# Moving ten groups of score tiles one place later in the projection stage of a Perceiver layer

## The chip, the cores and the metric

One Trainium2 chip, one of its NeuronCores. The metric is the time of one execution on the device in microseconds (us), the median of several runs. The engines are TensorE (PE; its weight loads are listed as PEld), VectorE (DVE), ScalarE (ACT), GpSimd (POOL) and SyncE (SP), which here only issues DMAs.

## The reference, cut to what matters

The input x is 512 x 512, the context ctx_768 is 8192 x 384. The layer is a cross attention, a local self attention and a feed-forward network with weights rounded to a 4-bit grid, each added to x. The change lies in the first part of the cross attention and in what the kernel does beside it:

```python
def _L0_xattn_ref(x, y, Wq, bq, Wk, bk, Wv, bv, W1, b1, W2, b2):   # y = ctx_768: 8192 rows
    q = (x @ Wq + bq)...                                           # 16 heads of 32 columns
    k = (y @ Wk + bk)...
    v = (y @ Wv + bv)...
    scores = jnp.einsum('bnhd,bmhd->bhnm', q, k) * scale
    attn = jax.nn.softmax(scores, axis=-1)                         # needs a bound of each row's maximum
    ...
def fp4_quant_dequant(x):                                          # for the weights of the last part
    scale = jnp.maximum(jnp.max(jnp.abs(xb), axis=-1, keepdims=True) / 6.0, 1e-12)   # blocks of 16
    q = _GRID[jnp.searchsorted(_MID, jnp.abs(xb / scale))] * jnp.sign(xb / scale) * scale
```

## The kernel before

The kernel is one program with explicit semaphores: each engine has its own list of instructions in a fixed order, and waits (`wait`, `wait_ge`) for counts that other engines raise. The first stage, "project" (lines 285 to 825), computes keys and values for 8192 context rows in 16 blocks (b = 0 to 15) of 512 rows; `two_blocks(i)` handles b = 2i (u = 0, an even block) and b = 2i + 1 (u = 1, an odd block). All operands are split into a high and a low float16 half, so that each product is three matmuls.

For one block TensorE issues, in this order: `keys` (L736): four tiles g = 0 to 3 of nine matmuls (L752); `next_y` (L777): twelve transposes (L710) of the next block's rows into the three PSUM banks of `yT_ps`; `values` (L759): four tiles t = 0 to 3 of nine matmuls (L769 to L771).

Between these stand groups of four "score tiles" (`maxima` of TensorE, L720, matmuls at L732): scores of 128 queries each against 512 keys of an earlier block, of which only the row maxima are wanted. The first three go to the three banks of `yT_ps`, the fourth to `pre_ps`; VectorE's own `maxima` (L646, reductions at L651) reads them out. A table `part_at` says at which place a group stands: KEYS_2 (behind the third key tile), VALUES_1, VALUES_2, VALUES_3 (behind the second, third and fourth tile of values). Twelve blocks, 2 to 4 and on, have a group at VALUES_1; blocks 3, 8 and 10 have a second one, at VALUES_3; block 15 has its two at KEYS_2 and VALUES_2. All groups share the same four banks. So before a group TensorE waits for three things: the stored keys (`k_out`, or `k_in`), `ylo_ready` (VectorE has taken the low half of the next block out of `yT_ps`, `y_low`, L611), and `pre_read`: VectorE has read all tiles of all earlier groups (`done_before`). `next_y` waits for `pre_read` too, for the three tiles in `yT_ps` (L779).

VectorE's list for one block is: four times the low half of a key tile (`key_low`, L607), with three steps of the weight rounding between them and, where the block before had a group at VALUES_3, two of that group's maxima behind each of the first two; `y_low`; two rounding steps (`quantize(2)`, L683); `maxima` of VALUES_1 (L684); two more rounding steps in an even block, three in an odd one (L687). The fifteen rounding steps of two blocks are listed in STEPS (L654): for each of three weight units w: `scales` (L616 to L622), `halves` of the unit before (L642, L643), `rounder` (L627, L629), `add` (L632), `subtract` (L636), and at last `halves` of unit 2. In an even block these are scales 0, rounder 0, add 0 between the keys, subtract 0 and scales 1 before the maxima, halves 0 and rounder 1 behind them; in an odd block add 1, subtract 1, scales 2 between the keys, halves 1 and rounder 2 before the maxima, add 2, subtract 2, halves 2 behind them.

GpSimd does two operations for each unit: `qn` (L497), started by the end of scales and awaited by rounder, and `w_whole` (L503), started by subtract and awaited by halves and by the next unit's scales (L619). ScalarE takes the high halves out of PSUM: `keys_out` (L539, L541), `y_high` (L548), `values_out` (L555). SyncE's queue stores keys, values and rounded weights and loads the next rows; a store of a weight unit waits for `halved` (L430).

Behind the stage stands the attention stage ("attend", from line 850), which begins when the maxima of the first head are complete.

Of the kernel before, what the change touches and what calls it, by code (L numbers as in the profile page):

```python
# [43 lines left out]
NB = M // BLK  # L44
# [87 lines left out]
def perceiver(nc, a, out):  # L132

    with ExitStack() as whole:
# [113 lines left out]
        def layer_norm_vector(dve, chain, var_ready, sd_ready, k, xn, xn_ready, first=0, tiles=range(TT)):  # L248


            for t in range(first, TT):
                chain(nc.vector.bn_stats(stats[:, t, :], x[:, t, :]))
            chain.wait()
            for t in range(TT):
                chain(nc.vector.bn_aggr(mv[:, t, :], stats[:, t, :]))
            chain.wait()
            nc.vector.tensor_scalar(ve[:], mv[:, :, 1], EPS, None, ALU.add).then_inc(var_ready, 1)
            dve.wait_ge(sd_ready, k)
            dve.wait_ge(var_ready, k)
            chain.link(nc.vector.reciprocal(r0[:], sd[:]))  # L260
            chain.link(nc.vector.tensor_tensor(r1[:], r0[:], r0[:], ALU.mult))
            chain.link(nc.vector.tensor_tensor(r2[:], r1[:], ve[:], ALU.mult))
            chain.link(nc.vector.tensor_scalar(r1[:], r2[:], -0.5, 1.5, ALU.mult, ALU.add))
            chain.link(nc.vector.tensor_tensor(r2[:], r0[:], r1[:], ALU.mult))
            for t in tiles:
                nc.vector.tensor_scalar(xn[:, t, :], x[:, t, :], mv[:, t, 0:1], r2[:, t:t + 1],  # L266
                                        ALU.subtract, ALU.mult).then_inc(xn_ready, 1)
# [17 lines left out]
        with ExitStack() as st:  # L285
# [71 lines left out]
            KEYS_2, VALUES_1, VALUES_2, VALUES_3 = range(4)  # L357
            part_at = {(2, VALUES_1): (0, 0), (3, VALUES_1): (0, 1), (3, VALUES_3): (0, 2), (8, VALUES_3): (1, 0),
                       (10, VALUES_3): (1, 1)}
            for b in range(4, NB - 1):  # L360
                part_at[b, VALUES_1] = (0, b - 1)
            part_at[NB - 1, KEYS_2] = (0, NB - 2)
            part_at[NB - 1, VALUES_2] = (0, NB - 1)
            done_before = {at: TT * n for n, at in enumerate(sorted(part_at))}
# [3 lines left out]
            def pre_bank(j):  # L368

                return yT_ps[:, j] if j < TT - 1 else pre_ps[:]  # L370
# [218 lines left out]
            def _(dve):  # L589
# [13 lines left out]
                def key_low(i, u, g):  # L603
                    n = (2 * i + u) * G + g
                    wait(dve, kf_ready, n + 1)
                    wait(dve, khi_ready, n + 1)
                    nc.vector.tensor_tensor(k_lo[:, u, g], kf[:, g % 2], k_hi[:, u, g], ALU.subtract).then_inc(klo_ready, 1)  # L607

                def y_low(i, u):
                    wait(dve, yhi_ready, 2 * i + u + 2)  # L610
                    nc.vector.tensor_tensor(yT_lo[:, 1 - u], yT_ps[:], yT_hi[:, 1 - u], ALU.subtract).then_inc(ylo_ready, 1)  # L611
# [34 lines left out]
                def maxima(b, place, tiles=range(TT)):  # L646
                    if (b, place) in part_at:
                        h, part = part_at[b, place]
                        for j in tiles:
                            dve.wait_ge(pre_ready, done_before[b, place] + j + 1)  # L650
                            nc.vector.tensor_reduce(part_max[:, h, j, part:part + 1], pre_bank(j), AX.X,  # L651
                                                    ALU.max).then_inc(pre_read, 1)
# [6 lines left out]
                def two_blocks(i, last):  # L659
                    steps = iter(STEPS)  # L660

                    def quantize(count):
                        for _ in range(count):
                            part, w = next(steps)
                            part(i, w)

                    def keys(u):
                        b = 2 * i + u
                        for g in range(G):
                            key_low(i, u, g)  # L670
                            if g < 3:
                                quantize(1)
                            maxima(b - 1, VALUES_3, range(2 * g, min(2 * g + 2, TT)))
                        maxima(b, KEYS_2)

                    for u in range(2):
                        if not (last and u == 1):
                            keys(u)
                            if i == 0 and u == 0:
                                dve.wait_ge(x_in, 16)  # L680
                                layer_norm_vector(dve, chain, var_ready, sd_ready, 1, xn_q, xn_ready)
                            y_low(i, u)
                            quantize(2)  # L683
                            maxima(2 * i + u, VALUES_1)  # L684
                            if last:
                                keys(1)
                            quantize(2 + u)  # L687
                            if last:
                                quantize(5)
                                maxima(2 * i + 1, VALUES_2)  # L690
                    assert next(steps, None) is None

                two_blocks(0, False)
                for g in range(G):
                    dve.wait_ge(qf_ready, g + 1)
                    dve.wait_ge(qhi_ready, g + 1)
                    nc.vector.tensor_tensor(q_lo[:, g], qf[:, g], q_hi[:, g], ALU.subtract).then_inc(qlo_ready, 1)
                for i in range(1, NB // 2):
                    two_blocks(i, i == NB // 2 - 1)
# [1606 lines left out]
```

## Time and profile before

| | us |
|---|---|
| median of 3 runs | 1385.35 |
| lowest of them | 1385.23 |
| profiled execution, span from first to last instruction | 1383.2 |
| TensorE busy in the span | 1332.2 |
| VectorE busy | 1120.9 |
| ScalarE busy | 806.1 |
| GpSimd busy | 778.7 |

The profiled execution is given by its span; the median lies 2.15 us above it, which is what lies around the span. An engine's matmuls overlap, so their printed durations (0.38 us) are longer than the distance from one start to the next. In a timeline the bracket at a row's end is the time for which the engine was idle before it and what released it; "issue" is a wait for which the profile shows no releaser.

### The profile page before, as it was taken

To read this page: it belongs to the slowest core of one execution; us is meant where nothing else is said; L and a number is where in the kernel's file an instruction comes from. 1 tells how busy PE (TensorE), PEld (TensorE's weight loads), DVE (VectorE), ACT (ScalarE), POOL (GpSimd) and SP (SyncE) were. 2 spreads that over 40 slices of the span, in tenths; PEclk is the share of its full clock that TensorE was granted. 3 is DMA by queue.
4 is the path that set the end of the run, shared out by engine and by line. 5 is a ranking of instruction groups with operands and counts; after the bars stand their busy time and mean duration, and the time that the engine had idled before them with its cause. 6 is when DMAs were issued, how large, how long until landed. Compare 5 with 4: busy or idle time off the path is not lost. (4 is left out here: it accounts for less than half of the span.)

```text
span 1383.2 us, 39979 instructions
## 1 busy us (share of the span) xinstructions
PE 1332.2 (96%) x17098; PEld 702.8 (51%) x17098; DVE 1120.9 (81%) x1786; ACT 806.1 (58%) x1459; POOL 778.7 (56%) x320
## 2 busy tenths in 40 slices
PE   7999999998999999999999999999999999999898
PEld 4444444443555555555555555545555445566454
DVE  5778888887888888888888888888887746578895
ACT  4454444443777777776777776776777841354332
POOL 0322222122899988988998898899889100201121
PEclk9999999999999999999999999999999999999999
DMA  8568777786352122122212112211210030491000
GB/s 265 177 169 231 207 211 211 210 238 177 91 183 69 39 69 67 30 65 67 69 39 68 56 38 69 67 50 57 59 66 31 5 145 1 92 214 41 0 9 23
DMA packets 127799, 137.54 MB, mean 99 GB/s; under 512 B 44995, under 2 KB 108995, under 8 KB 125699
## 3 DMA queue, kind: packets, MB, share of 16 engines
q1 hardware_dynamic: 127622, 134.98, 34.6%
q8 instruction: 135, 2.21, 0.7%
q14 instruction: 42, 0.34, 0.1%
HBM read 75.70 MB, written 44.17 MB: 87 GB/s over the span
## 5 line engine op out<-in xcount | busy, mean ns | idle before, releaser
L1297 DVE TENSOR_REDUCE early<-attend_banks 128x1 f32<-128x512 f32 x952 | 612.4, 685 | 80.8 <-PE attend_banks L1042 75.6
L1261 ACT ACTIVATE attend_prob<-attend_banks 128x512 f32<-128x512 f32 x1024 | 536.0, 599 | 200.8 <-PE attend_banks L1079 198.6
L1439 POOL TENSOR_TENSOR early<-early,attend_prob 128x1024 f32<-128x1024 f32 x210 | 614.5, 2926 | 37.7 <-ACT attend_prob L1261 9.6
L1079 PE MATMUL attend_banks<-early,k_first 97*32 97x512 f16 x2560 | 258.9, 382 | 3.1 <-ACT attend_prob L1261 3.1
L1042 PE MATMUL attend_banks<-k_first,early 96*32 96x512 f16 x2272 | 235.1, 382 | 1.1 <-PEq L285 1.1
L1079 PE MATMUL attend_banks<-early,attend_k_rest 97*32 97x512 f16 x1536 | 154.1, 381 | 2.8 <-ACT attend_prob L1261 2.8
L1042 PE MATMUL attend_banks<-attend_k_rest,early 96*32 96x512 f16 x1536 | 155.8, 380 | 0.0
L1103 PE MATMUL attend_banks<-attend_prob,ones 128*32 128x128 f32 x3048 | 134.3, 272 | 3.6 <-DVE attend_recip L1309 3.6
L1092 PE MATMUL attend_banks<-attend_prob,wkv_area 128*32 128x512 f32 x1024 | 134.1, 592 | 0.0
L1092 PE MATMUL attend_banks<-attend_prob,attend_vh_odd 128*32 128x512 f32 x1024 | 133.6, 592 | 0.0
L503 POOL TENSOR_TENSOR project_w_whole<-project_grid,project_qscale 128x704 f32<-128x704 f32 x24 | 33.3, 1386 | 173.0 <-DVE project_grid L636 173.0
L1103 PEld LDWEIGHTS attend_banks<-attend_prob,ones 128*32 128x32 f32 x3048 | 95.6, 110 | 54.5 <-DVE attend_recip L1309 11.1
L1079 PEld LDWEIGHTS attend_banks<-early,k_first 97*32 97x32 f16 x2560 | 77.3, 97 | 85.6 <-ACT attend_prob L1261 46.6
L1042 PEld LDWEIGHTS attend_banks<-k_first,early 96*32 96x32 f16 x2272 | 71.3, 97 | 58.4 <-issue 34.9
L555 ACT ACTIVATE project_v<-project_v_ps 128x512 f32<-128x512 f32 x64 | 38.1, 597 | 92.1 <-PE project_v_ps L771 92.1
L497 POOL TENSOR_TENSOR project_qn<-early,project_qinv 128x704 f32<-128x704 f32 x24 | 37.9, 1580 | 87.6 <-issue 50.2
L539 ACT ACTIVATE early<-project_k_ps,project_bk 128x512 f32<-128x512 f32 x64 | 44.0, 688 | 63.6 <-PE project_k_ps L752 61.6
L769 PE MATMUL project_v_ps<-project_w_hi,project_yT_hi 128*128 128x512 f16 x192 | 73.9, 385 | 5.7 <-ACT project_v L555 5.7
L1079 PEld LDWEIGHTS attend_banks<-early,attend_k_rest 97*32 97x32 f16 x1536 | 47.0, 96 | 57.8 <-ACT attend_prob L1261 38.1
L752 PE MATMUL project_k_ps<-project_yT_hi,project_w_hi 128*128 128x512 f16 x192 | 72.5, 379 | 2.3 <-ACT project_q_hi L574 1.4
L770 PE MATMUL project_v_ps<-project_w_lo,project_yT_hi 128*128 128x512 f16 x192 | 73.9, 385 | 0.0
L771 PE MATMUL project_v_ps<-project_w_hi,project_yT_lo 128*128 128x512 f16 x192 | 73.7, 384 | 0.0
(220 smaller groups left out, 1823.6 us busy)
## 6 DMA issues: line engine op xcount, KB each, us to landing
v_scratch<-project_v SPq DMA_DIRECT2D x16, 1024.0 KB, 8.9
early<-in_ctx_dram SPq DMA_DIRECT2D x16, 768.0 KB, 6.2
k_first<-k_scratch SPq DMA_DIRECT2D x36, 256.0 KB, 3.5
k_scratch<-project_k_hi SPq DMA_DIRECT2D x64, 128.0 KB, 2.9
k_scratch<-project_k_lo SPq DMA_DIRECT2D x64, 128.0 KB, 3.1
attend_vh_odd<-v_scratch SPq DMA_DIRECT2D x8, 1024.0 KB, 5.0
wkv_area<-v_scratch SPq DMA_DIRECT2D x7, 1024.0 KB, 4.8
attend_k_rest<-k_scratch SPq DMA_DIRECT2D x24, 256.0 KB, 3.5
```

Source lines behind the costliest of these rows:

```text
L539: nc.scalar.activation(kf[:, g % 2], k_ps[:, g % 2], ACT.Identity, bias=bk[:, g:g + 1], scale=1.0 / WSCALE).then_inc(kf_ready, 1)
L752: last = nc.tensor.matmul(k_ps[:, g % 2], (w_lo if p == 2 else w_hi)[:, 0, k, cols], (yT_lo if p == 1 else yT_hi)[:, u, k], start=(k, p) = ...
L769: nc.tensor.matmul(v_ps[:, t % 2], yT_hi[:, u, k, cols], w_hi[:, 1, k], start=k == 0, stop=False)
L770: nc.tensor.matmul(v_ps[:, t % 2], yT_hi[:, u, k, cols], w_lo[:, 1, k], start=False, stop=False)
L771: last = nc.tensor.matmul(v_ps[:, t % 2], yT_lo[:, u, k, cols], w_hi[:, 1, k], start=False, stop=k == CK - 1)
L1042: last = nc.tensor.matmul(pre_ps[c * HD:(c + 1) * HD, bank, :], q_stack[0:KROWS, h, queries], keys_at(s, part * BLK, (part + 1) * BLK)[0:K ...
L1079: last = nc.tensor.matmul(s_ps[c * HD:(c + 1) * HD, s_bank[n], :], key_rows[:, c * HD:(c + 1) * HD], q_stack[0:KROWS + 1, h, :], start=Tru ...
L1092: last = nc.tensor.matmul(pv_ps[t * HD:(t + 1) * HD, :], vh[s][:, BT * q + t, :], prob[:, q % PSLOTS, t, :], start=q == 0, stop=q == QUADS ...
L1103: last = nc.tensor.matmul(den_ps[t * HD:(t + 1) * HD, 0:P], ones[:], prob[:, q % PSLOTS, n, t * P:(t + 1) * P], start=q == 0 and n == summ ...
L1261: nc.scalar.activation(prob[:, q % PSLOTS, t, :], s_ps[:, s_bank[BT * q + t]], ACT.Exp, scale=SCALE).then_inc(p_ready, 1)
L1297: nc.vector.tensor_reduce(part_max[:, s, j, part:part + 1], pre_ps[:, bank], AX.X, ALU.max).then_inc(pre_read, 1)
L1439: nc.gpsimd.tensor_tensor(sums, sums, prob[:, q % PSLOTS, 0:n], ALU.add).then_inc(pool_summed, 1)
```

## The change

The groups at VALUES_1 in blocks 4 to 13 go to VALUES_2, so that TensorE issues them behind the third tile of values instead of the second. On VectorE their maxima go behind the block's last rounding steps, at the end of its list. The group of block 14 stays at VALUES_1, as do those of blocks 2 and 3, and the groups at VALUES_3 in blocks 3, 8 and 10 stay where they are.

```diff
             part_at = {(2, VALUES_1): (0, 0), (3, VALUES_1): (0, 1), (3, VALUES_3): (0, 2), (8, VALUES_3): (1, 0),
                        (10, VALUES_3): (1, 1)}
-            for b in range(4, NB - 1):
-                part_at[b, VALUES_1] = (0, b - 1)
+            for b in range(4, NB - 2):
+                part_at[b, VALUES_2] = (0, b - 1)
+            part_at[NB - 2, VALUES_1] = (0, NB - 3)
             part_at[NB - 1, KEYS_2] = (0, NB - 2)
             part_at[NB - 1, VALUES_2] = (0, NB - 1)
...
                             quantize(2 + u)
+                            if not last:
+                                maxima(2 * i + u, VALUES_2)
                             if last:
                                 quantize(5)
                                 maxima(2 * i + 1, VALUES_2)
```

## Rows read from the trace of the kernel before

**Rows 1.** Windows: the projection stage and the rest. Columns: us, busy of each engine.
```profile
core 0: us, PE busy (x) PEld busy (x) DVE busy (x) ACT busy (x) POOL busy (x), PEclk, DMA share, GB/s
0.00:343.00 343.00, 316.00 (x1514) 155.51 (x1514) 270.30 (x418) 157.10 (x228) 76.38 (x54) 0.99 0.73 209
343.00:1383.20 1040.20, 1016.17 (x15584) 547.29 (x15584) 850.65 (x1368) 648.96 (x1231) 702.34 (x266) 1.00 0.23 63
```

**Rows 2.** Timeline of TensorE, blocks 5 to 9. Columns: start us, us, operation, idle before.
```profile
137.28 1.47 PE L710 MATMUL project_yT_ps<-ident,early 128*128 128x128 f32 x12
...
155.09 1.47 PE L710 MATMUL project_yT_ps<-ident,early 128*128 128x128 f32 x12
...
161.32 0.81 PE L732 MATMUL project_yT_ps<-k_first,early 96*128 96x512 f16 x3 [0.87 <-issue]
...
191.65 1.47 PE L710 MATMUL project_yT_ps<-ident,early 128*128 128x128 f32 x12
...
203.55 0.81 PE L732 MATMUL project_yT_ps<-k_first,early 96*128 96x512 f16 x3 [0.76 <-DVE early L651]
```

**Rows 3.** Timeline of VectorE, blocks 6 and 8.
```profile
159.47 1.75 DVE L611 TENSOR_TENSOR project_yT_lo<-project_yT_ps,project_yT_hi 128x1536 f16<-128x1536 f32 x1
...
200.92 1.88 DVE L651 TENSOR_REDUCE early<-project_yT_ps 128x1 f32<-128x512 f32 x3
202.72 0.68 DVE L651 TENSOR_REDUCE early<-project_pre_ps 128x1 f32<-128x512 f32 x1
203.31 0.52 DVE L642 TENSOR_SCALAR project_w_out<-project_w_whole 128x704 f16<-128x704 f32 x1
...
204.68 0.52 DVE L627 TENSOR_SCALAR project_qr<-project_qn 128x704 uint32<-128x704 uint32 x1
205.24 0.53 DVE L629 TENSOR_SCALAR project_qr<-project_qr 128x704 f32<-128x704 f32 x1
207.95 0.69 DVE L607 TENSOR_TENSOR project_k_lo<-early,project_k_hi 128x512 f16<-128x512 f32 x1 [2.19 <-ACT project_k_hi L541]
```

**Rows 4.** Timeline of VectorE and GpSimd, block 0, which has no score tiles.
```profile
35.48 0.52 DVE L642 TENSOR_SCALAR project_w_out<-project_w_whole 128x704 f16<-128x704 f32 x1
36.03 1.96 DVE L643 SCALAR_TENSOR_TENSOR project_w_out<-project_w_whole,project_w_out 128x704 f16<-128x704 f32 x1
37.91 0.52 DVE L627 TENSOR_SCALAR project_qr<-project_qn 128x704 uint32<-128x704 uint32 x1
38.46 0.53 DVE L629 TENSOR_SCALAR project_qr<-project_qr 128x704 f32<-128x704 f32 x1
39.02 0.69 DVE L607 TENSOR_TENSOR project_k_lo<-early,project_k_hi 128x512 f16<-128x512 f32 x1
...
35.70 1.54 POOL L497 TENSOR_TENSOR project_qn<-early,project_qinv 128x704 f32<-128x704 f32 x1 [1.11 <-issue]
```

**Rows 5.** Timeline of VectorE and GpSimd, block 7.
```profile
171.55 0.69 DVE L607 TENSOR_TENSOR project_k_lo<-early,project_k_hi 128x512 f16<-128x512 f32 x1 [0.45 <-ACT project_k_hi L541]
172.16 0.89 DVE L636 TENSOR_TENSOR project_grid<-project_qs,project_qr 128x704 f32<-128x704 f32 x1
173.46 1.60 DVE L607 TENSOR_TENSOR project_k_lo<-early,project_k_hi 128x512 f16<-128x512 f32 x1 [0.42 <-ACT project_k_hi L541]
...
175.89 0.19 DVE L620 TENSOR_SCALAR project_qscale<-project_amax 128x44 f32<-128x44 f32 x1
...
173.12 1.39 POOL L503 TENSOR_TENSOR project_w_whole<-project_grid,project_qscale 128x704 f32<-128x704 f32 x1 [7.15 <-DVE project_grid L636]
```

**Rows 6.** Timeline of VectorE and GpSimd, block 6: both want to start.
```profile
154.25 0.68 DVE L607 TENSOR_TENSOR project_k_lo<-early,project_k_hi 128x512 f16<-128x512 f32 x1
...
154.47 1.71 POOL L497 TENSOR_TENSOR project_qn<-early,project_qinv 128x704 f32<-128x704 f32 x1 [3.92 <-issue]
```

**Rows 7.** TensorE's clock behind two gaps: timeline row, then windows (columns as in rows 1).
```profile
29.58 0.50 PE L769 MATMUL project_v_ps<-project_w_hi,project_yT_hi 128*128 128x512 f16 x1 [4.96 <-ACT project_v L555]
...
29.58:33.22 3.64, 3.64 (x9) 1.32 (x10) 3.64 (x6) 0.43 (x1) 0.02 (x1) 0.53 1.03 207
115.93:117.86 1.93, 0.00 (x1) 0.03 (x1) 1.86 (x5) 1.27 (x2) 0.00 (x0) 1.00 0.92 348
117.86:121.95 4.09, 4.09 (x17) 2.71 (x18) 2.94 (x5) 1.45 (x1) 0.00 (x0) 0.58 0.07 19
```

## The prediction

> **What bounds the kernel now.** I read the windows by stage first: the change touches only the first 343 us, and there TensorE is busy for 316.0 us, VectorE for 270.3 [rows 1]. Everything behind it, 1040 us, starts when this stage ends and should only slide. Next comes TensorE's timeline, read from one block's transposes to the next: 137.28 to 155.09 is 17.81 us, the floor of a block, in which TensorE never stops (76 matmuls and twelve transposes). From 155.09 to 191.65 two blocks take 36.56, which is 0.94 over two floors [rows 2]. The excess is the gap at 161.32, ahead of the VALUES_1 group of block 6. Its releaser is printed as "issue", but VectorE's timeline names it: y_low of that block runs from 159.47 to 161.22, and the group starts 0.1 us later [rows 3]. I find this gap in the even blocks 6, 8, 10, 12 and 14; the odd ones and block 4 have next to none. Blocks 8 and 10 have one more gap of the same size ahead of VALUES_3; the row of block 8 is shown, released by VectorE's maxima [rows 2]. So TensorE bounds the stage, with VectorE less than 1 us behind it, once every two blocks.
>
> **Part 1, the four matmuls move behind the third value tile.** Nothing is added. A matmul takes (17.81 - 1.4) / 76 = 0.216 us from start to start, with 1.4 us for the transposes, so nine take 1.94 us, more than the 0.94 us for which TensorE waited for y_low; so that wait goes in blocks 6, 8, 10 and 12, with 1.0 us of slack. Block 14 keeps its place and its wait. The keys that the group needs were stored a block earlier and are no later wait. The wait of next_y for the banks has some 3 us to spare: in block 5 the maxima would end just before VectorE's next key_low, ahead of the transposes at 155.09 [rows 2].
>
> **Part 2, the four maxima move to the end of VectorE's block.** The reductions themselves cost the same: 203.31 - 200.92 = 2.39 us [rows 3]. But in even blocks they stood between scales 1 and halves 0, beside GpSimd's qn. Without them halves 0 meets qn. Block 0 has no score tiles and shows just this order: L642 at 35.48, L643 at 36.03 takes 1.96 us, until GpSimd's qn is done at 37.24, and rounder and the rest end at 39.02 [rows 4]. So from the end of scales to the end of rounder are 39.02 - 35.48 = 3.54 us. In block 8 the same work takes 205.24 + 0.56 - 203.31 = 2.49 us. VectorE's list of an even block grows by 1.05 us. If L643 were not held up and only rounder waited for qn, it would be about 0.3: bounds 0.3 and 1.05, and I take the row with the same order. In odd blocks halves 2 waits for GpSimd's w_whole in both orders and the sum stays. SyncE's stores of units 0 and 2 get their `halved` earlier, 1.3 to 2.4 us; nothing of this stage's path hangs on them.
>
> **Part 3, what this does in blocks 8 and 10.** The VALUES_3 group waits for all earlier tiles to be read. Before, the maxima it waits for began at 200.92 and TensorE resumed at 203.55 [rows 2, 3]. Now they begin after halves 0 and rounder 1, 3.54 us later. This instant hangs on VectorE's list alone, whatever TensorE gained: +3.54 us for each of the two blocks, 7.08 in all. Behind the waiting matmuls in TensorE's queue stand all keys of the next block, for which ScalarE and then VectorE wait; VectorE already stood idle for 2.19 us there [rows 3], so it cannot make anything good.
>
> **Part 4, blocks 6 and 12.** Here a gap really goes, 0.94 us, but VectorE must keep up. In block 7 key_low g=1 waited 0.45 us [rows 5]. VectorE comes 1.05 us later, and k_hi comes 0.94 earlier, so the first key_low starts some 0.7 later than before and g=1 and subtract 1 some 0.35 later. The next key_low (173.46) no longer waits 0.42 us, and starts right behind subtract, before GpSimd's w_whole does. Before, it started second and took 1.60 instead of 0.69 us [rows 5]. Where key_low starts first, as at 154.25, it takes 0.68 and GpSimd's operation is stretched from 1.39 to 1.71 [rows 6]. By this w_whole ends about 2.75 us after subtract's start and the L620 that waits for it comes at 2.82; before it came 175.89 - 172.16 = 3.73 after. That is 0.91 gained against 0.35 lost: the pair ends 0.55 us earlier. Ends: +0.38 if key_low were again held up, -0.94 if VectorE costs nothing. Two such pairs (6 and 7, 12 and 13): -1.10 us.
>
> The Trainium skill, "SBUF — State Buffer", section "Who interferes with whom", says that a VectorE operation with two SBUF inputs and a GpSimd operation that reads SBUF exclude each other, and that whoever issues first holds the ports for its whole length. The trace agrees in both directions [rows 4 to 6]. If the rule did not hold for the key_low of block 7, the sum would be 1.9 us higher.
>
> **Part 5, TensorE's clock.** The gap ahead of VALUES_3 is 0.92 us: the printed 0.76, and the 0.38 of the matmul before less 0.216 [rows 2]. In block 8 TensorE would now wait 0.92 + 0.94 + 0.94 (gained in blocks 6 and 8) + 3.54 - 0.55 = 5.8 us, in block 10 0.92 + 0.94 + 3.54 = 5.4 us. Both gaps of such a kind in this stage were followed by half clock: behind 4.96 us of idling the granted clock is 0.53 for 3.64 us, and behind 1.93 us it is 0.58 for 4.09 us [rows 7]. That is the 1.2 GHz level. In the first, nine matmuls took 3.64 instead of 9 x 0.216 = 1.94 us: 1.70 us lost. Gaps of 0.9 us had no such effect. I add 2 x 1.70 = 3.40; ends 0 and 4.
>
> The Trainium skill, "TensorE: Matmul & The Clock Gate", section "HAM oscillation — how this bites in real kernels", warns that waits which recur can send the array back to its slow clock each time. Had its rule no force here, the 3.40 us would be missing; the two rows speak for it.
>
> **Sum.** 7.08 - 1.10 + 3.40 = +9.4 us: the span of 1383.2 becomes 1392.6, and with the 2.15 us around it 1394.7 us. Against 1385.35 that is 0.7%, far inside the 2% that a measurement of this kernel can tell from no change.
>
> **The rivals.** *The clock stays up*: for it speaks that no half clock follows the gaps of 0.9 us; against it both longer gaps [rows 7]. 7.08 - 1.10 = +6.0: 1391.3 us. Chance 0.15. *VectorE loses little*: L643 is not held up, so that the waits of blocks 8 and 10 grow by 2.77 each and blocks 6 and 12 give their full 0.94; 5.54 - 1.88 + 3.40 = +7.1, 1392.4 us, or 1389.0 with full clock. Block 0 speaks against it. Chance 0.10. *VectorE falls behind*: key_low of blocks 7 and 13 is again held up, 7.08 + 0.76 + 3.40 = +11.2, 1396.6 us; more would need stalls that I don't see. Chance 0.10. *The other side, faster*: the y_low waits go and nothing takes their place. The place is the VALUES_3 group of blocks 8 and 10, and it decides whether VectorE has read the moved tiles when TensorE gets there, at about 200.8. Then four gaps go, -3.8 us: 1381.6. For it speaks that TensorE is the bound and all four gaps are real; against it, VectorE was only starting on those tiles at 200.92 in the earlier order. Chance 0.05.
>
> **How the numbers follow.** The forecast has 0.60 and by itself reaches from 1393 to 1396.5. The range takes in the rivals but the fast one: 1388 to 1397.5. All cases lie within 2%; for more in either direction I leave 0.01 and 0.02.
>
> **What would show it right or wrong.** The two gaps ahead of VALUES_3 should be 5 to 6 us with VectorE's L651 as releaser and half clock behind them; the gaps ahead of the moved groups gone; L643 of even blocks near 1.96 us; the L607 of block 7 that took 1.60 near 0.7; the distance between transposes 17.8 us from block 6 to 7; the one in block 14 still there; and the attention stage as long as before. Gaps under 2 us ahead of VALUES_3 would overturn it.

## The result

The changed kernel takes 1394.6 us in the median of 5 runs (1393.0 to 1396.1); the kernel before takes 1385.35. One of the five runs of the kernel before took 2734.39 us and has no part in the ratio. The ratio is 1.0065 with a 95% interval of 1.0053 to 1.0078: slower by two thirds of a percent, clear of noise, and within the 2% that counts as no change. 1394.7 us had been forecast. The profiled execution is the fastest of the five, 1393.0 us with a span of 1391.2, 8.0 us above the profiled one of before.

The timeline of TensorE, changed kernel. The columns are start us, us, operation, and in brackets the idle time before it with its releaser (all line numbers behind the table `part_at` are higher by one to three in this kernel: L713 is the transpose, L735 the score tile). Blocks 6, 7, 8 and 9 begin their transposes at the four L713 rows:

```profile
154.44 1.47 PE L713 MATMUL project_yT_ps<-ident,early 128*128 128x128 f32 x12
...
172.15 1.47 PE L713 MATMUL project_yT_ps<-ident,early 128*128 128x128 f32 x12
...
189.87 1.47 PE L713 MATMUL project_yT_ps<-ident,early 128*128 128x128 f32 x12
...
205.91 1.44 PE L735 MATMUL project_yT_ps<-k_first,early 96*128 96x512 f16 x3 [5.93 <-DVE early L652]
...
216.81 1.50 PE L713 MATMUL project_yT_ps<-ident,early 128*128 128x128 f32 x12 [0.50 <-issue]
...
250.15 1.44 PE L735 MATMUL project_yT_ps<-k_first,early 96*128 96x512 f16 x3 [5.48 <-DVE early L652]
...
321.19 0.81 PE L735 MATMUL project_yT_ps<-k_first,early 96*128 96x512 f16 x3 [1.54 <-issue]
```

Against [rows 2] the reader sees three things. From block 6 to 7 the distance is 17.71 us instead of 18.75: the gap at 161.32 is gone. The VALUES_3 group of block 8, which had 0.76 us of idle time in its bracket, has 5.93, and that of block 10 has 5.48, both released by VectorE's maxima. And block 14, whose group was not moved, has 1.54 us where it had 0.87 (row at 321.19).

VectorE in block 8, changed kernel; the last two rows are GpSimd in block 8 and VectorE in block 9:

```profile
199.74 0.52 DVE L643 TENSOR_SCALAR project_w_out<-project_w_whole 128x704 f16<-128x704 f32 x1
200.29 1.96 DVE L644 SCALAR_TENSOR_TENSOR project_w_out<-project_w_whole,project_w_out 128x704 f16<-128x704 f32 x1
202.17 0.51 DVE L628 TENSOR_SCALAR project_qr<-project_qn 128x704 uint32<-128x704 uint32 x1
202.72 0.53 DVE L630 TENSOR_SCALAR project_qr<-project_qr 128x704 f32<-128x704 f32 x1
203.28 1.89 DVE L652 TENSOR_REDUCE early<-project_yT_ps 128x1 f32<-128x512 f32 x3
...
205.09 0.68 DVE L652 TENSOR_REDUCE early<-project_pre_ps 128x1 f32<-128x512 f32 x1
...
199.96 1.54 POOL L498 TENSOR_TENSOR project_qn<-early,project_qinv 128x704 f32<-128x704 f32 x1 [1.11 <-issue]
...
211.89 0.69 DVE L608 TENSOR_TENSOR project_k_lo<-early,project_k_hi 128x512 f16<-128x512 f32 x1 [6.12 <-ACT project_k_hi L542]
```

This is the sequence of block 0 [rows 4], to 0.01 us: 1.96 for L644, which had 0.89 in block 8 before (a row at 203.87), and 203.28 - 199.74 = 3.54 us from the end of scales to the first maximum, which used to be zero. TensorE resumes 0.14 us after the last maximum ends. VectorE then waits 6.12 us for the keys of block 9, where it had waited 2.19 [rows 3].

The windows over TensorE's two long waits and the stretches behind them, changed kernel (us, busy and number of rows of PE, PEld, DVE, ACT, POOL, granted clock, DMA share, GB/s):

```profile
205.91:209.50 3.59, 3.59 (x10) 1.28 (x11) 0.00 (x0) 0.00 (x0) 0.00 (x0) 0.54 1.04 375
...
250.15:253.80 3.65, 3.65 (x10) 1.29 (x11) 0.00 (x0) 0.00 (x0) 0.00 (x0) 0.53 1.04 365
351.67:1391.20 1039.53, 1015.83 (x15584) 539.80 (x15584) 850.54 (x1368) 648.90 (x1231) 701.58 (x266) 1.00 0.23 63
```

Behind each wait the clock granted is 0.54 and 0.53: the 1.2 GHz level, as behind the 4.96 us at the start [rows 7]. The last row is everything behind the projection stage: 1039.5 us against 1039.9 before.

**Where the 8.0 us of the two profiled executions are.** The stage from the transposes of block 5 to the first matmul of the attention stage takes 351.67 - 136.72 = 214.95 us instead of 343.26 - 137.28 = 205.98: +8.97 us. The rest is not the change's: +1.12 before block 3; -1.67 in block 4, where the same wait of 1.93 us was followed by half clock in the one execution [rows 7] and not in the other (shown in the section on the hardware); and -0.41 behind the stage.

### The profile page after: what moved, and what is told of

The parts are those of the page before. It is cut to its first block and busy times, and to the rows that moved or that the text cites. A ratio compares the mean times of both kernels' runs of the same rounds, so it can differ in the third digit from the quotient of the medians.

```text
span 1391.2 us, 39979 instructions
## 1 busy us (share of the span) xinstructions
PE 1333.8 (96%) x17098; PEld 696.4 (50%) x17098; DVE 1124.3 (81%) x1786; ACT 805.8 (58%) x1459; POOL 779.6 (56%) x320
```

## The experiments

Whole times are given as ratios to the kernel before, run on the same chip as the experiment, since the chips differ a little: it took 1386.59 us on the chip of the first three experiments and of the kernel with 44 extra matmuls, 1386.08 on that of the kernel with 23 and of the last kernel of all, and 1385.93 on that of the other two. The resolution of a ratio is about 0.1%, 1.4 us. The terms in question are of that size, so each experiment is also read by its own trace, from one block's transposes to the next. This table puts those distances side by side, in us, each from TensorE's timeline of that kernel:

| | before | after | 8, 10 left | 8, 10 only | TensorE only | busy 44 | busy 23 |
|---|---|---|---|---|---|---|---|
| block 6 to 7 | 18.75 | 17.71 | 17.72 | 18.75 | 17.72 | 17.71 | 17.72 |
| block 7 to 8 | 17.81 | 17.72 | 17.71 | 17.81 | 17.72 | 17.72 | 17.72 |
| block 8 to 9 | 21.22 | 26.94 | 21.83 | 26.79 | 23.04 | 29.07 | 25.23 |
| block 10 to 11 | 21.23 | 26.56 | 21.38 | 26.63 | 23.06 | 29.07 | 24.82 |
| block 12 to 13 | 18.75 | 17.72 | 17.71 | 18.75 | 17.72 | 17.71 | 17.72 |
| block 5 to attention | 205.98 | 214.95 | 204.80 | 216.97 | 207.00 | 219.69 | 212.39 |

### Blocks 8 and 10 left where they were

The edit is against the changed kernel.

```diff
-            for b in range(4, NB - 2):
-                part_at[b, VALUES_2] = (0, b - 1)
-            part_at[NB - 2, VALUES_1] = (0, NB - 3)
+            for b in range(4, NB - 1):
+                part_at[b, VALUES_1 if b in (8, 10, NB - 2) else VALUES_2] = (0, b - 1)
```

> Blocks 8 and 10 keep their group at VALUES_1 on both engines; the other eight groups stay moved. My theory: the whole loss sits in blocks 8 and 10, where the VALUES_3 group waits for moved maxima. Without it the gaps ahead of VALUES_3 are 0.8 us again, no half clock follows them, and what is left is the gain of blocks 6 and 12, together 1.1 us: 1384.2 us. Rival: late maxima cost VectorE 1.05 us in every even block and delay TensorE everywhere: at least 1387 us, with gaps in blocks 6 and 12. Rival: the full 0.94 us is gained in each of the two: 1383.5 us.

Measured: ratio 0.9982, interval 0.9973 to 0.9991, which is faster than before by 2.5 us (1.2 to 3.7). From block 5 to the attention stage it is 204.80 us, 1.18 less than before, where 1.1 had been expected; the 2.5 us of the medians are more than the stage accounts for, and only the low end of their interval meets it. The gaps ahead of VALUES_3 are back (timeline of TensorE, blocks 8 and 10; the first row of each pair is the VALUES_1 group):

```profile
197.23 0.81 PE L734 MATMUL project_yT_ps<-k_first,early 96*128 96x512 f16 x3 [1.47 <-issue]
202.90 0.81 PE L734 MATMUL project_yT_ps<-k_first,early 96*128 96x512 f16 x3 [0.76 <-DVE early L651]
...
236.35 0.81 PE L734 MATMUL project_yT_ps<-k_first,early 96*128 96x512 f16 x3 [1.02 <-issue]
242.03 0.81 PE L734 MATMUL project_yT_ps<-k_first,early 96*128 96x512 f16 x3 [0.76 <-DVE early L651]
```

So the loss sits in blocks 8 and 10, and the other eight moves are a small gain. The 1.47 instead of 0.87 us ahead of VALUES_1 of block 8 is VectorE's lag out of block 6, carried to the next place where TensorE waits for it: of the 1.1 us gained in blocks 6 and 7, 0.6 come back there. Ahead of block 14's group, behind the moved block 12, there are 1.53 us in the same way. Block 10, whose even neighbour 8 was not moved, has 1.02 and so next to none of this.

### Only blocks 8 and 10 moved

The edit is against the kernel above.

```diff
-                part_at[b, VALUES_1 if b in (8, 10, NB - 2) else VALUES_2] = (0, b - 1)
+                part_at[b, VALUES_2 if b in (8, 10) else VALUES_1] = (0, b - 1)
```

> Only the groups of blocks 8 and 10 are moved. My theory: 2 x 3.54 us of later VALUES_3 and 2 x 1.70 us of half clock, nothing gained elsewhere: +10.5, 1395.8 us, with gaps of about 5.4 us ahead of VALUES_3 in both blocks. Rival, the loss is spread over all ten blocks: about two tenths of it, 1387 us.

Measured: ratio 1.0083, interval 1.0068 to 1.0097, +11.5 us (9.4 to 13.4); in the trace +10.99 from block 5 to the attention stage. TensorE in the two blocks:

```profile
207.70 1.44 PE L734 MATMUL project_yT_ps<-k_first,early 96*128 96x512 f16 x3 [5.35 <-DVE early L651]
...
252.38 1.44 PE L734 MATMUL project_yT_ps<-k_first,early 96*128 96x512 f16 x3 [5.34 <-DVE early L651]
```

Two moves of ten make more than the whole loss, and the two experiments together give it back to within 0.8 us: 10.99 - 1.18 = 9.8 us, against 8.97 with all ten. From the transposes of block 6 to VALUES_3 of block 8 they add up: 52.02 us here and 47.93 in the kernel above, 3.56 more and 0.53 less than the 48.46 before, and 3.01 more with all ten. What mostly doesn't is the half clock: from the group in block 8 to the next transposes are 219.03 - 207.70 = 11.33 us here, 2.01 more than before, where the changed kernel has 1.58 more; in block 10 it is 1.85 here and 1.64 there.

### TensorE's order alone

The edit is against the changed kernel, as are those of the kernels kept busy below.

```diff
                             maxima(2 * i + u, VALUES_1)
+                            maxima(2 * i + u, VALUES_2)
...
                             quantize(2 + u)
-                            if not last:
-                                maxima(2 * i + u, VALUES_2)
```

> TensorE's order as in the changed kernel, VectorE's as in the kernel before (maxima behind scales 1). My theory: VectorE's place is what costs. VALUES_3 of block 8 then resumes when it did before, less the 0.94 us gained in block 6; the gaps ahead of it are about 2.8 us in block 8 and 1.9 in block 10; L643 takes 0.89 us again. -1.9 us: 1383.5 us with full clock, up to 1386.9 if half clock follows both gaps. Rival, TensorE's order is at fault (matmuls too close to VALUES_3): the time stays near 1394 us.

Measured: ratio 1.0004, interval 0.9993 to 1.0014. With VectorE's maxima in their old place, eight of the nine microseconds are gone (207.00 instead of 214.95 us in the table), so it is VectorE's order that costs most of them, and the rival is out. The waits ahead of VALUES_3 are 1.9 us in both blocks; I had 2.8 for block 8, having counted the gain of block 6 a second time, although here VectorE comes that much earlier too. Half clock follows both. So TensorE's order is not free in these two blocks: the last kernel of this section, which has the same orders but leaves the groups of blocks 8 and 10 where they were, takes 203.74 us in the stage, 3.26 less. Without that cost this kernel would be ahead of the one before, which takes 205.98:

```profile
202.31 0.81 PE L734 MATMUL project_yT_ps<-k_first,early 96*128 96x512 f16 x3 [1.93 <-DVE early L652]
...
202.31:206.00 3.69, 3.69 (x11) 1.41 (x12) 2.15 (x4) 0.00 (x0) 0.00 (x0) 0.59 0.80 163
243.12:247.00 3.88, 3.88 (x12) 1.46 (x13) 2.14 (x4) 0.00 (x0) 0.00 (x0) 0.61 0.94 210
```

### TensorE kept busy in the two waits

```diff
+                        if place == VALUES_3 and b in (8, 10):
+                            pe.wait_ge(khi_ready, G * (b + 1))
+                            keep_busy(k_ps[:, 0], 44)
                         wait(pe, pre_read, done_before[b, place])
```

> The changed kernel, with 44 extra matmuls of the identity into a free bank in the two waits ahead of VALUES_3 of blocks 8 and 10, some 0.11 us each, 4.9 us in all, less than the waits last. My theory: half clock behind the two waits costs 1.70 us each, and goes: 1391.2 us, with VALUES_3 resuming no later. Rival, the clock is no part of it: 1394.6 us.

Measured: ratio 1.0095, interval 1.0080 to 1.0109, slower still. I had read the duration of a `keep_busy` matmul wrongly: a timeline row counts two for each float32 matmul of the program, so that one takes 0.22 us and 44 take 9.8, longer than the wait. The bracket ahead of VALUES_3 is empty, and the kernel is slow through its own filling. The arithmetic does fit (26.94 + 9.8 - 5.9 - 1.7 = 29.1, measured 29.07), but what was wanted is the wait unchanged and the clock alone different. So again with 23 of them:

> As the kernel with 44 extra matmuls, which took 9.8 us instead of the 4.9 us that I had set, so that they ended behind the wait. Now 23 of them, 0.223 us each as measured there, 5.1 us in the two waits of 5.9 and 5.5 us. If half clock behind the waits costs what the trace of the changed kernel suggests, VALUES_3 still resumes on VectorE's maxima, the granted clock behind it is 1.00, and block 8 to 9 takes 26.94 - 1.7 = 25.2 us, the whole 3.4 us less than the changed kernel: a ratio of about 1.004 to the kernel before. Rival, the clock costs nothing: 26.9 us and the ratio 1.0065.

```profile
198.36 5.30 PE L276 MATMUL project_k_ps<-ident 128*128 128x128 f32 x46
204.35 0.82 PE L738 MATMUL project_yT_ps<-k_first,early 96*128 96x512 f16 x3 [0.69 <-DVE early L652]
...
204.35:208.00 3.65, 3.65 (x17) 1.66 (x18) 0.00 (x0) 0.63 (x2) 0.00 (x0) 1.00 1.03 369
246.91:250.50 3.59, 3.59 (x17) 1.67 (x18) 0.00 (x0) 0.57 (x1) 0.00 (x0) 1.00 0.97 346
```

The 23 matmuls are 46 in the row. Now VALUES_3 still waits for VectorE, the granted clock behind it is 1.00, and in the same stretch TensorE has 17 rows instead of 10. Block 8 to 9 takes 25.23 us, and 25.2 had been expected: half clock cost 1.71 us there and 26.56 - 24.82 = 1.74 in block 10. The whole time shows it only weakly: ratio 1.0055, interval 1.0039 to 1.0071, which holds both the expected 1.004 and the 1.0065 of the rival. In this profiled execution 0.9 of the 3.4 us are lost again behind block 14, where a wait for a store of keys is 1.35 us. By the blocks the cost of the clock is shown; by the median it isn't.

### Can the gain be had without the loss?

Three kernels try it. In the first, VectorE's maxima stay in their old place, as in the kernel with TensorE's order alone, and in the table only TensorE's part of blocks 4, 6 and 12 moves. The edits of all three are against the kernel before; the line of VectorE's `maxima` at VALUES_2, right behind that at VALUES_1, is left out here:

```diff
+                part_at[b, VALUES_2 if b in (4, 6, 12) else VALUES_1] = (0, b - 1)
```

> Only TensorE's four matmuls of the groups of blocks 4, 6 and 12 move behind the third tile of values; VectorE's order is that of the kernel before everywhere, and blocks 8 and 10 are untouched. My theory: the waits for y_low in blocks 6 and 12 go at no cost, 2 x 0.94 us: 1383.5 us, with L643 at 0.89 us and no gap in blocks 6 and 12. Rival, VectorE was about to become the bound and takes part of it back: 1384.3 us.

Measured: ratio 0.9991, interval 0.9983 to 1.0000. From block 5 to the attention stage it is 204.39 us, 1.59 less than before, between the 1.88 of the theory and the 1.05 of the rival. Block 6 to 7 takes 17.71 us, but block 7 to 8 takes 18.05, for this reason (VectorE and GpSimd in block 7 of this kernel, then TensorE's VALUES_1 group):

```profile
172.27 0.88 DVE L636 TENSOR_TENSOR project_grid<-project_qs,project_qr 128x704 f32<-128x704 f32 x1
173.33 1.84 DVE L607 TENSOR_TENSOR project_k_lo<-early,project_k_hi 128x512 f16<-128x512 f32 x1 [0.18 <-ACT project_k_hi L541]
...
173.23 1.39 POOL L503 TENSOR_TENSOR project_w_whole<-project_grid,project_qscale 128x704 f32<-128x704 f32 x1 [6.36 <-DVE project_grid L636]
...
179.24 0.81 PE L733 MATMUL project_yT_ps<-k_first,early 96*128 96x512 f16 x3 [0.17 <-issue]
```

VectorE waits 0.18 us for the keys and so starts 0.1 us after GpSimd; its operation takes 1.84 us. In the changed kernel VectorE is later, doesn't wait, and goes first:

```profile
171.88 0.88 DVE L637 TENSOR_TENSOR project_grid<-project_qs,project_qr 128x704 f32<-128x704 f32 x1
172.68 0.69 DVE L608 TENSOR_TENSOR project_k_lo<-early,project_k_hi 128x512 f16<-128x512 f32 x1
...
174.71 0.19 DVE L621 TENSOR_SCALAR project_qscale<-project_amax 128x44 f32<-128x44 f32 x1 [0.56 <-POOL project_w_whole L504]
...
172.84 1.77 POOL L504 TENSOR_TENSOR project_w_whole<-project_grid,project_qscale 128x704 f32<-128x704 f32 x1 [7.27 <-DVE project_grid L637]
```

The second kernel adds block 14 to the table, and:

```diff
-                values(i, 0, range(2))
+                values(i, 0, range(3))
                 keys(i, 1)
-                values(i, 0, range(2, BT))
+                values(i, 0, range(3, BT))
```

and the same for ScalarE's `values_out`.

> The last kernel, and in block 14 three tiles of values stand before the keys of block 15 instead of two, on TensorE and ScalarE, so that its group can stand behind the third. My theory: the gap of 0.94 us in block 14 goes too, 1382.5 us, if the keys of block 15, now 1.94 us later, don't delay the last maxima. Rival: the stage ends with the stored keys of block 15 and VectorE's last maxima, so that the later keys cost as much: 1384 us or more.

Measured: ratio 0.9987, interval 0.9978 to 0.9996. The gap in block 14 goes, and comes back 8 us before the stage's end, where TensorE waits for the stored keys of block 15: 2.72 us instead of the 1.35 of the first of these kernels. From block 14's transposes to the attention stage are 36.96 us, in that kernel and in the kernel before the change 36.82. The rival was right: that gap is worth nothing.

```profile
334.25 0.82 PE L733 MATMUL project_yT_ps<-k_first,early 96*128 96x512 f16 x3 [2.72 <-DMA k_scratch<-project_k_lo]
```

The third moves TensorE's groups in all ten blocks but 8 and 10 and leaves VectorE's order as it was:

> TensorE's groups moved in all of the ten blocks but 8 and 10, VectorE's maxima in their old place everywhere. The gains of blocks 6 and 12 and nothing against them: blocks 6 to 8 and 12 to 14 at 17.72 us each, as where all ten were moved; the gaps ahead of VALUES_3 at 0.8 us. Blocks 5 to 14 in 167.0 us, 2.2 us less than before, 1.0016 times faster, level with or 0.3 us ahead of the kernel in which both engines' parts move. Rival, the early maxima in odd blocks wait for TensorE's now later matmuls and VectorE falls behind: 168 us or more.

In the stage it does what was expected: blocks 6 to 8 and 12 to 14 take 17.71 to 17.72 us each, blocks 5 to 14 take 166.81 (169.16 before), and from block 5 to the attention stage are 203.74 us, 2.24 less than before and the best of all. In block 7 key_low starts at 172.94 here, 0.04 us ahead of GpSimd instead of 0.1 behind it, and takes 0.69 us, which is what the first of the three kernels missed. Yet the ratio is 0.9992, interval 0.9983 to 1.0001, which holds both the expected gain and none at all. The section on the hardware shows where the rest is in the profiled execution. Of the kernels tried, the one with blocks 8 and 10 left and the one with block 14 beat both the kernel before and the changed one beyond their intervals; which of the four small gains is the largest, these runs can't tell.

## Why the prediction was right

**The waits for y_low.** Forecast: gone in four blocks, 0.94 us each, and 1.0 us of slack. Measured: 18.75 to 17.71 us in block 6; the group starts 0.92 us behind the end of y_low in block 6 and 0.42 in block 8, so the slack is smaller where VectorE lags, but wasn't used up in either. The odd blocks, taken as the floor at 17.81, turned out to hold 0.09 us of the same wait and went to 17.72; the floor was wrong by so much, and a wait for y_low was 1.04 us and not 0.94.

**VALUES_3 in blocks 8 and 10.** Forecast: 3.54 us later, fixed by VectorE's list alone, less the lag term. From the transposes of block 6 to the group in block 8 are 205.91 - 154.44 = 51.47 us, before 203.55 - 155.09 = 48.46 [rows 2]: +3.01, forecast 3.54 - 0.55 = 2.99. In block 10, where nothing was gained before, the same distance from the transposes of block 9 grows by 3.55. The two experiments on blocks 8 and 10 and the one with TensorE's order alone make this the cause and not only a fitting number. The waits themselves are 5.93 and 5.48 us in their brackets, 6.1 and 5.6 in the prediction's count, which adds 0.16; forecast were 5.8 and 5.4. The floor explains most of the difference: up to this place TensorE had gained 2.2 us in block 8, not 1.88.

**L643 held up by GpSimd.** Forecast 1.96 us from block 0, measured 1.96; the rival that had it free is out, and so is the fast one, since TensorE had to wait ahead of VALUES_3.

**Blocks 6 and 12 against VectorE's lag.** Forecast: each pair 0.55 us earlier, because the low half of a key tile starts ahead of GpSimd and takes 0.7 instead of 1.60 us. Measured: it takes 0.69 us, and GpSimd's operation is stretched from 1.39 to 1.77; from subtract to L621, which waits for that operation, are 174.71 - 171.88 = 2.83 us, forecast 2.82. By the rule of "SBUF — State Buffer" in the Trainium skill, section "Who interferes with whom", whoever issues first holds the ports, and the two fences of block 7 above, where the first is ahead by no more than 0.16 us and VectorE's durations are 1.15 us apart, show it both ways round. What a pair of blocks gains on TensorE is more, and VectorE's lag takes a part back at the next wait for VectorE: of 1.12 us in blocks 12 and 13, 0.67 come back ahead of block 14's group, 1.54 instead of 0.87 us, which leaves 0.45. In block 8, ahead of VALUES_3, the pair's gain is 3.54 - 3.01 = 0.53. Forecast were 0.55.

**The clock.** Forecast 1.70 us for each of two waits. From the group to the transposes of block 9 are 216.81 - 205.91 = 10.90 us instead of 9.32, +1.58, and +1.64 in block 10; against the kernel that was kept busy 1.71 and 1.74. With only blocks 8 and 10 moved it was 2.01 and 1.85, so that 1.70 is no constant. The rival with full clock, 1391.3 us, is out.

**Sum.** 9.4 us forecast, 8.97 in the stage, 9.3 in the medians. The terms hold to some tenths of a microsecond each. That the last digit of 1394.7 fits is luck: the runs of the changed kernel spread over 3.1 us.

## What to carry to other kernels

A group that is moved later on the engine that bounds is safe only up to the next instruction that waits for all groups before it. Look for a wait on a running count, and ask which engine's list, with everything now ahead of the moved part, sets when that count is reached. Move the producer alone first: here TensorE's four matmuls could go later for nothing outside blocks 8 and 10, while VectorE's maxima had a reader that was already waiting. And a longer wait can cost more than its length, through the clock behind it: TensorE's waits of 0.8 us ahead of VALUES_3 had full clock behind them, those of 1.9 us and of 5.3 to 5.9 us half clock.

## What the runs showed of the hardware

**The same wait can be followed by half clock or by full clock.** In block 4, up to which all ten kernels issue the same instructions, TensorE waits 1.92 to 1.94 us in each. Before, the window behind it was granted 0.58 [rows 7]; in the changed kernel, for the same work:

```profile
118.97:123.00 4.03, 4.03 (x25) 2.60 (x26) 3.60 (x5) 2.00 (x2) 0.00 (x0) 1.00 0.06 18
```

The window ends before block 4's own group. From these transposes to the next are 19.42 or 19.43 us in seven of the ten traces and 17.75 in three (the changed kernel, TensorE's order alone, 23 extra matmuls). The group of block 4 is moved in all three, and in five of the seven. So the same instructions and the same wait give 1.7 us or nothing. In the kernel with TensorE's order alone both waits of 1.9 us in blocks 8 and 10 were followed by half clock; the waits of 1.54 us in block 14 of the changed kernel and of 1.47 in block 8 of the kernel with blocks 8 and 10 left were not.

**The attention stage begins at full clock or with a few microseconds of half clock.** The first 10 us of it in three kernels that are alike from there on (before; blocks 8 and 10 left; TensorE's order without 8 and 10), one window row each:

```profile
343.26:353.26 10.00, 10.00 (x148) 4.62 (x152) 8.38 (x14) 6.89 (x13) 4.06 (x2) 0.83 0.96 279
```

```profile
342.05:352.05 10.00, 10.00 (x168) 4.36 (x172) 9.30 (x16) 7.95 (x16) 5.50 (x2) 1.00 0.96 277
```

```profile
341.62:351.62 10.00, 10.00 (x120) 4.43 (x124) 7.49 (x12) 6.45 (x12) 3.41 (x1) 0.69 1.00 281
```

In 10 us TensorE issues 148, 168 and 120 matmuls. In the first row the clock granted is 0.50 in the window from 344.76 to 346.26 and 1.00 from 347.76 on, in the last 0.50 up to 347.62. The last kernel reaches the attention stage 0.43 us before the second, and from there to the end needs 1042.6 us against 1039.5. What TensorE does ahead of that point is the same in these two, waits of 1.6 and 1.1 us, so this is a difference between executions as far as these profiles show; whether a kernel's own timing shifts the odds stays open. It isn't the only one behind the stage: over the ten traces that part takes 1038.3 to 1043.8 us, and the longest of them, with blocks 8 and 10 only, began at 0.83 as the kernel before did with 1039.9. Such differences are as large as any gain that was looked for here. They account for the 2.2 us in the profiled execution; that they hide them in the medians too is likely but not shown.
